# Filter taps built by half steps, one spectrum turn moved behind a scaling, and the last output tile written in four blocks

## What is computed

```
x = x + 0.5 * ffn(layernorm(x))
x = x + attn(layernorm(x))
x = x + 0.5 * ffn(layernorm(x))

ffn(x):  h = silu(x W1' * s1) * (x W2' * s2)        # ternary weights, 256 -> 1024
         h = gelu(h H1' * t1);  h = gelu(h H2' * t2)  # 1024 -> 1024
         return h W3' * s3                            # 1024 -> 256
attn(x): K = 2 Re sum_n C_n exp(dtA_n * t)            # S4D filter, 256 channels x 1024 taps
         y = irfft(rfft(x, 2048) * rfft(K, 2048))[:1024]
         return gelu(y) W' + b
```

## Time and profile before

| what | value |
|---|---|
| median of 3 runs | 1461.65 us (1461.04 to 1462.56) |
| the profiled execution's own time | 1463.29 us |
| its span in the trace | 1461.0 us |
| TensorE busy | 1437.8 us, 98% of the span |
| VectorE busy | 986.4 us, 68% |
| ScalarE busy | 476.6 us, 33% |
| GpSimd busy | 48.1 us, 3% |
| mean granted TensorE clock | 0.998 |

### The profile page before, as it was taken

One profiled execution on the slowest core, in us unless ns is written; L12 is line 12 of the kernel. 1 busy time (PEld: TensorE's weight loads), 2 busy tenths in 40 slices (PEclk: granted clock), 3 DMA queues, 4 the chain that ended last, 5 costly groups with the idle time before them and its releaser, 6 DMA issues.

```text
span 1461.0 us, 17259 instructions
## 1 busy us (share of the span) xinstructions
PE 1437.8 (98%) x6910; PEld 1159.7 (79%) x6910; DVE 986.4 (68%) x1729; ACT 476.6 (33%) x721; POOL 48.1 (3%) x42
## 2 busy tenths in 40 slices
PE   7999999999999999999999999999999999999998
PEld 3688888878777778787887887878878788888886
DVE  7676877684777887858878577784787754353432
ACT  3724342333324324223242242422424223141321
POOL 0000100000000000010000100001000010000000
PEclk9999999999999999999999999999999999999999
DMA  9000000002114121031210312013120112010000
GB/s 362 15 1 29 29 30 29 15 30 72 40 44 144 44 87 55 14 130 44 87 33 26 126 59 72 19 54 97 59 73 15 58 40 72 0 44 0 30 0 16
DMA packets 52545, 80.27 MB, mean 55 GB/s; under 512 B 2672, under 2 KB 44528, under 8 KB 50928
## 3 DMA queue, kind: packets, MB, share of 16 engines
q1 hardware_dynamic: 52464, 79.15, 16.1%
HBM read 57.12 MB, written 22.02 MB: 54 GB/s over the span
## 4 chain that ended last, share of the span: by engine, by line
PE 92%; DVE 6%; ACT 1%; issue 1%; DMA 0%; POOL 0%; DVEq 0%; ACTq 0%; POOLq 0%
PE ps L1249 76%; PE ps L1311 8%; PE ps L1344 3%; PE ps L1397 2%; PE ps L1240 1%; DVE hid_b_lo L1175 1%; PE ps L1338 1%; PE ps L1339 1%; DVE pt L829 1%; PE ps L1387 0%; DVE hid_b_hi L1173 0%; ACT act_o L476 0%; DVE low L1140 0%; DVE tab L832 0%; DVE gr L832 0%
## 5 line engine op out<-in xcount | busy, mean ns | idle before, releaser
L476 ACT ACTIVATE act_o<-ps,scales 128x512 f32<-128x512 f32 x384 | 264.2, 689 | 908.1 <-PE ps L1249 905.3
L1249 PE MATMUL ps<-hid_b_hi,h 128*128 128x512 f32 x1024 | 404.4, 395 | 0.5 <-DVE hid_b_lo L1175 0.3
L1249 PE MATMUL ps<-hid_b_lo,h 128*128 128x512 f32 x1024 | 401.6, 392 | 0.0
L1249 PE MATMUL ps<-hid_a_hi,h 128*128 128x512 f32 x992 | 393.1, 396 | 0.2
L1249 PE MATMUL ps<-hid_a_lo,h 128*128 128x512 f32 x992 | 388.7, 392 | 0.0
L1249 PEld LDWEIGHTS ps<-hid_b_hi,h 128*128 128x128 f32 x1024 | 192.5, 188 | 44.8 <-DVE hid_b_lo L1175 1.4
L1249 PEld LDWEIGHTS ps<-hid_b_lo,h 128*128 128x128 f32 x1024 | 192.5, 188 | 43.1 <-issue 1.2
L1249 PEld LDWEIGHTS ps<-hid_a_hi,h 128*128 128x128 f32 x992 | 186.3, 188 | 47.5 <-DVE hid_a_lo L1166 2.8
L1249 PEld LDWEIGHTS ps<-hid_a_lo,h 128*128 128x128 f32 x992 | 186.4, 188 | 41.4 <-issue 2.2
L1249 PE MATMUL ps<-hid_b_hi,w 128*128 128x512 f32 x480 | 190.3, 396 | 2.1 <-DVE gz L1226 2.1
L1249 PE MATMUL ps<-hid_b_lo,w 128*128 128x512 f32 x480 | 189.6, 395 | 0.0
(11 more groups left out here) (246 smaller groups left out, 1237.9 us busy)
## 6 DMA issues: line engine op xcount, KB each, us to landing
ks<-k_d SPq DMA_DIRECT2D x32, 512.0 KB, 3.8
raws<-in_weights SPq DMA_DIRECT2D x11, 1024.0 KB, 15.5
gz<-in_x SPq DMA_DIRECT2D x8, 512.0 KB, 3.7
xin<-in_x SPq DMA_DIRECT2D x8, 512.0 KB, 3.9
x_d<-xin SPq DMA_DIRECT2D x8, 512.0 KB, 2.9
z_d<-xin SPq DMA_DIRECT2D x8, 512.0 KB, 2.9
k_d<-ks SPq DMA_DIRECT2D x8, 512.0 KB, 2.6
zb<-z_d SPq DMA_DIRECT2D x8, 512.0 KB, 5.2
```

The lines of the kernel that those rows point to most:

```text
L476: A(act_o[:, k % ACT_SLOTS], bank(source), func, scale=scale).then_inc(s_act, 1)
L1249: last = MM(o, weight[:, k, cols].bitcast(dt), part[:, k].bitcast(dt), start=(k == 0 and i == 0), stop=(k == n - 1 and i == len(act_) - 1))
```

## The change

1. `MADE` is replaced by `TABLES` and `FACTORS`: the two halves of a piece (the table, the factors) now stand at steps of their own, and `make_factors` is split into `make_table` and `make_factors`. `MASKED` and `MULTIPLIED` move with them. The last multiplication is at step 21 of tile 3 instead of 17, and so is the copy-out of the sums (L581) with the SyncE transfers behind it. The next tile's norm in tile 3 is at steps 19 and 20 instead of 17 and 18.
2. `turn(7)` stands behind the scaling L1226 of tile 4, ahead of the addition L1230. `finish_taps(7)` stands behind the first silu of tile 5.
3. Tile 15's last layer is `layer_three_last`. Its four sums go to banks 4 to 7, one per block, and it does not wait for step 23's activation but for the filter's last use of these banks. Blocks 0 and 1 run their first seven k-steps before anything that needs step 23. VectorE then scales and adds each block by itself (128x256), and SyncE stores each block by itself (128 KB).

```
-    if T == 3:
-        return 17, 18
-    if T == 4:
+    if T in (3, 4):
         return 19, 20
...
-MADE = {(2, 17): 0, (2, 19): 1, (2, 21): 2, (3, 8): 3, (3, 9): 4, (3, 10): 5, (3, 11): 6, (3, 14): 7}
-MULTIPLIED = {(2, 20): 0, (2, 22): 1, (3, 8): 2, (3, 11): 3, (3, 12): 4, (3, 13): 5, (3, 14): 6, (3, 17): 7}
+TABLES = {(2, 17): 0, (2, 19): 1, (2, 21): 2, (2, 23): 3, (3, 9): 4, (3, 11): 5, (3, 15): 6, (3, 17): 7}
+FACTORS = {(2, 18): 0, (2, 20): 1, (2, 22): 2, (3, 8): 3, (3, 10): 4, (3, 14): 5, (3, 16): 6, (3, 18): 7}
+MULTIPLIED = {(2, 21): 0, (2, 23): 1, (3, 8): 2, (3, 11): 3, (3, 13): 4, (3, 17): 5, (3, 19): 6, (3, 21): 7}
...
-            store_x(ALL - 1)
-            sp.wait_ge(s_xst, 16 * ALL)
+            for j in range(J):
+                sp.wait_ge(s_x, ALL + j)
+                sp.dma_start(rows(out, TILES - 1)[:, j], xin[:, j]).then_inc(s_xst, 16)
+            sp.wait_ge(s_xst, 16 * (ALL - 1 + J))
...
-                if T == 3 and k == 17:
+                if T == 3 and k == 21:
                     act.wait_ge(s_tap, PIECES)
...
                 for m in range(KH):
                     hidden(T, m, ACT.Silu, scales[:, 0, m:m + 1])
+                    if T == 5 and m == 0:
+                        finish_taps(7)
...
                 if T == 4:
-                    for i in (6, 7):
-                        finish_taps(i)
+                    finish_taps(6)
...
-                if (T, k) in MADE:
-                    make_factors(MADE[T, k])
+                if (T, k) in TABLES:
+                    make_table(TABLES[T, k])
+                if (T, k) in FACTORS:
+                    make_factors(FACTORS[T, k])
...
+            def make_table(n):
+
+                if n >= 2:
+                    dve.wait_ge(s_tap, n - 1)
+                step(powers_product(tab[:, n % 2], n, uim, ure, 0))
+
+            def make_factors(n):
+
+                if n:
+                    dve.wait_ge(s_masked, n)
+                powers_product(gr[:, :, :], n, ure, uim, 1).then_inc(s_factor, 1)
...
                 if T == 4:
                     turn(6)
-                    turn(7)
...
+                if T < ALL - 1:
+                    dve.wait_ge(s_o, T + 1)
+                    V.tensor_tensor(gz[:, :, :], bank(2, 2).rearrange("p (j d) -> p j d", j=J),
+                                    s3[:, :].unsqueeze(1).to_broadcast([P, J, D]), ALU.mult).then_inc(s_upd, 1)
+                    if T == 4:
+                        turn(7)
...
+            dve.wait_ge(s_xr, 16 * ALL)
+            for j in range(J):
+                dve.wait_ge(s_o, ALL + j)
+                V.tensor_tensor(gz[:, j], ps[:, 4 + j, 0:D], s3[:, :], ALU.mult).then_inc(s_upd, 1)
+                dve.wait_ge(s_upd, ALL + j)
+                V.tensor_tensor(xin[:, j], xin[:, j], gz[:, j], ALU.add).then_inc(s_x, 1)
...
+            def layer_three_last(dt):
+
+                T = ALL - 1
+                pe.wait_ge(s_x2, B)
+
+                def steps_of(j, first, last_):
+                    for k in range(first, last_):
+                        pe.wait_ge(s_split, at_split(T, 2 * KH + k))
+                        for i, part in enumerate((hid_a_hi, hid_a_lo)):
+                            last = MM(ps[:, 4 + j, 0:D], part[:, k, j * P:(j + 1) * P].bitcast(dt), w3[:, k].bitcast(dt),
+                                      start=(k == 0 and i == 0), stop=(k == KH - 1 and i == 1))
+                    return last
+
+                for j in range(2):
+                    steps_of(j, 0, KH - 1)
+                for j in range(J):
+                    steps_of(j, KH - 1 if j < 2 else 0, KH).then_inc(s_o, 1)
```

More of the change, by code:

```diff
@@ L133, in norm2_at @@
     return (20, 21) if 4 < T <= TILES else (-1, -1)
[L138 to L140 removed]
+TABLES = {(2, 17): 0, (2, 19): 1, (2, 21): 2, (2, 23): 3, (3, 9): 4, (3, 11): 5, (3, 15): 6, (3, 17): 7}
+FACTORS = {(2, 18): 0, (2, 20): 1, (2, 22): 2, (3, 8): 3, (3, 10): 4, (3, 14): 5, (3, 16): 6, (3, 18): 7}
+MASKED = {(2, 19): 0, (2, 21): 1, (2, 23): 2, (3, 9): 3, (3, 11): 4, (3, 15): 5, (3, 17): 6, (3, 19): 7}
+MULTIPLIED = {(2, 21): 0, (2, 23): 1, (3, 8): 2, (3, 11): 3, (3, 13): 4, (3, 17): 5, (3, 19): 6, (3, 21): 7}
 def norm_calls():
@@ L810, in prepare, with powers_product @@
                     step(V.scalar_tensor_tensor(uim[:, 0], uim[:, 0], col(C_IM), xt[:, 1], ALU.mult, ALU.add))
-                if (T, k) in MADE:
-                    make_factors(MADE[T, k])
+                if (T, k) in TABLES:
+                    make_table(TABLES[T, k])
+                if (T, k) in FACTORS:
+                    make_factors(FACTORS[T, k])
             def lift(i):
                 return x12[:, i].unsqueeze(2).to_broadcast([P, P, NU])
-            def make_factors(n):
+            def powers_product(out_, n, x, y, i):
@@ L819, in make_factors @@
                 q = slice(n * PIECE, (n + 1) * PIECE)
                 wide = [P, PIECE, NU, NV]
[L821 to L836, removed]
+                out_, extra = (t.rearrange("p q (u v) -> p q u v", v=NV) for t in (out_, pt[:, :, :]))
@@ new lines, in powers_product @@
+                for to, u, v in ((out_, x, vre), (extra, y, vim)):
+                    last = V.tensor_tensor(to, u[:, i, q].unsqueeze(3).to_broadcast(wide),
+                                           v[:, i, q].unsqueeze(2).to_broadcast(wide), ALU.mult)
+                step(last)
+                return V.tensor_tensor(out_, out_, extra, ALU.add)
+            def make_table(n):
+                if n >= 2:
+                    dve.wait_ge(s_tap, n - 1)
+                step(powers_product(tab[:, n % 2], n, uim, ure, 0))
@@ L1222, in _ @@
                     update(second_of(T))
-                dve.wait_ge(s_o, T + 1)
                 if T == 0:
                     dve.wait_ge(s_s3, 1)
[L1226 to L1230, removed]
+                if T < ALL - 1:
[4 more added lines that the diff above has]
+                        turn(7)
+                    dve.wait_ge(s_upd, T + 1)
+                    dve.wait_ge(s_xr, 16 * (T + 1))
+                    V.tensor_tensor(xin[:, :, :], xin[:, :, :], gz[:, :, :], ALU.add).then_inc(s_x, 1)
+            dve.wait_ge(s_xr, 16 * ALL)
[4 more added lines that the diff above has]
+                V.tensor_tensor(xin[:, j], xin[:, j], gz[:, j], ALU.add).then_inc(s_x, 1)
         @block.tensor
@@ L1437, in feed_forward @@
                         project(second_of(T))
-                    layer_three(T, dt)
+                    if T + 1 < ALL:
+                        layer_three(T, dt)
+                layer_three_last(dt)
             pe.wait_ge(s_ident, 16)
```

## The result

The changed kernel takes 1454.45 us in the median of 4 runs (1453.2 to 1456.95), the kernel before 1462.1 us (4 runs, 1461.04 to 1462.56). The ratio is 0.9947, 95% interval 0.9936 to 0.9959: faster by 7.65 us, where 6.5 were forecast. Measured again beside its parts it is 1455.82 against 1462.47 us, 6.65 us.

What follows compares the result with a forecast made beforehand. TensorE, busy 98% of the span, bounds the kernel, so only its waits, slow stretches and the work behind its last matmul count. Taps 2.2, turn 0.8 and end 3.5 sum to 6.5 us: 1461.65 - 6.5 = 1455.1, range 1453.2 to 1457.3.

Steps and rivals of the forecast that it cites:

- Taps: Tile 3, steps 11 to 16: tap multiplications no longer wait for masks; gain 2.2 us, bounds 1.6 and 2.4.
- The cover of the mirror matmuls: Time between the tap sums' landing and the mirror matmuls needing them: shrinks from 16 us to 1.3 or more, costing nothing.
- Rival D: Mirror's input late, from 1.3 us of delay on: slower, 1464.6 us, chance 0.02; 0.04 that it takes part of the gain.
- The moved turn: Tile 5's start: the gap is cut in two, worth nothing by itself; clock saving 0.8 us, bounds 0 and 1.75.
- the slow stretch: Tile 5, behind TensorE's 2.09 us gap: granted clock 0.95 over 35 us, avoiding it saves up to 1.75 us.
- Rival A: Tile 5's start: the clock falls as before, behind the second gap; gain 5.7 us, time 1455.9, chance 0.3.
- The end: Last layer and store: 0.78 us from the wait, 1.62 from VectorE, 1.1 from the smaller store; 3.5 us together.
- Rival B: Last store: fixed cost takes its whole gain, or four issues delay the end; end gives 2.4, 1456.2 us, chance 0.1.
- Rivals C and E: C: tile 3's tap stalls stay, 1457.3 us, chance 0.05; E: a tap entry or last layer still waits, 1458.8, 0.03.
- The sum: Whole kernel: 2.2 + 0.8 + 3.5 = 6.5 us faster, 1455.1 us against the median.

Runs made afterwards that it cites:

- changed, again: The changed kernel with no edit, measured once more beside its parts: 1455.82 us, ratio 0.9955 to the kernel before.
- turn(7) moved: The changed kernel with turn(7) alone moved, in halves behind two gates of tile 5: 1454.44 us, ratio 0.9948 to the kernel before.

## Why the prediction was right, point by point

- **Taps.** 2.2 us forecast, 2.23 in the first profiles (89.03 to 86.80), 2.2 to 2.3 between kernels with and without the part. The halves fit because 3.11 us of VectorE stand against 3.665.
- **The cover of the mirror matmuls.** "1.3 or more" was forecast and 1.3 measured, by taking a step away. Rival D's mechanism is real and sat one step from deciding; its price was under-stated. The prediction has "each us late one us lost", but a wait of 2.34 us cost 2.9 to 3.5 by the tile, with the clock at half behind it.
- **The moved turn.** "The reordering by itself is worth nothing" holds within 0.1 us. The idle pieces were 0.52 and 1.44, forecast 0.5 and 1.8: the records show step 1 as 2.1 us of work where 1.83 was taken, and from its start to step 2's it was 3.56 us, forecast 3.62. In the profile the term was 1.5 us of the 1.75 (93.27 to 91.78), 1.3 of it the slow stretch. For the median 0.8 was taken, the middle between two values because nothing could decide; the part alone gave 0.75, with an interval of 0.3 to 2.9. That the two agree is luck and confirms no step of the reasoning. Rival A did not occur in any of the six profiles that have the two pieces, and the 2.09 us piece let the clock fall in two of three.
- **The end.** 0.78 and 1.62 us forecast; from the last gelu's start to VectorE's end there were 1457.69 - 1446.88 = 10.81 us before and 8.42 after, 2.39 less. For the store 1.1 was forecast and 1.2 measured where no engine was late. Rival B (the fixed cost eats the gain) falls with the two kernels that changed the stores alone. The Trainium skill's advice to coalesce many small transfers into one large (DMA: Bandwidth & Descriptors, "Rules for kernel authors") doesn't hold where the last transfer is on the path: 1.7 us from issue to landing for 128 KB against 2.9 for 512. And the "~2 µs" of fixed cost in the same page's "Latency and other measured facts" is too much here, where 128 KB took 1.7 us with its data; that is why the end gained 1.2 by the store and not the 0.9 which the prediction worked out from the page.
- **Rivals C and E.** No step of tile 3 is held up, and the last layer starts without a wait; both fall with the first profile after.
- **The sum.** 6.5 us forecast, 7.65 and 6.65 measured; both lie in the range. By the profiles the terms are 2.2 for the taps, 2.4 + 1.2 for the end and 0.1 for the reordering, 5.9 us, and 1.3 more in executions in which the slow stretch stood before. The medians are coarser than that: the three parts alone add up to 3.1 + 0.75 + 4.8 = 8.7 us, 2 us more than the whole measured beside them. So the terms are confirmed by the tiles and the end, and the sum only to 1 or 2 us.
- **What the prediction took wrongly.** It laid the spread of the timed runs to the slow stretch at tile 5. More of it is the clock at another place, the start. The stretch from the first transposes to those at the end of tile 0 took 94.0 to 96.0 us in the 13 profiles. TensorE starts at half its rate there, and how long that lasts differs: the first matmuls of 128x512 begin 0.85 us apart until 18.65 us in the kernel before and until 15.24 in "changed, again", and 0.43 apart from then on. TensorE's groups in 15 to 18 and in 15.6 to 18 us (count, busy us, mean ns):

```profile
L1249 PE MATMUL ps<-zf,raws 128*128 128x512 f32 x5 | 4.4, 1050 | 0.0
```
```profile
L1263 PE MATMUL ps<-zf,raws 128*128 128x512 f32 x7 | 3.3, 605 | 0.0
```

Each trace's first record of the full clock lies between 15.4 and 18.8 us, and the later it is, the longer is tile 0 (93.99 us with the earliest, 95.59 and 95.96 with the two latest). At half the rate 3.4 us more cost 1.7 of the 2.0 us between the extremes; "turn(7) moved" has besides 0.5 us more waiting for the first weights than the others. The late engine adds 1.6 to 2 us in two profiles.

## What to carry to other kernels

Where one engine is nearly always busy, look for what stands on another engine's queue ahead of the instruction it waits for, and ask for the next wait behind that one: cutting a gap in two by reordering is worth next to nothing by itself until the sum of the work ahead of the last of the waits falls; it can still keep the clock up: the clock fell in none of six profiles with the gap cut in two, and in two of three with the gap whole. Threaded side work fits if each piece plus the step's own work stays under the step's length; halves over more steps of 3.67 us did that at no cost for the taps, as long as their consumer was still behind them by more than a transfer, while the halves of turn(7) in steps of 1.84 us gave back 0.6 of 1.4 us. When executions of one kernel differ by a few us, compare them stretch by stretch, the start first. At a program's end, split the last scaling and store so that only the last block's are on the path.

## What was not expected of the hardware

The granted clock went to 0.5 behind a gap of only 2.09 us in two executions and stayed at 1.0 behind the same gap in a third; a gap of 2.34 us brought it down, two of 0.5 and 1.4 us with 2.1 us of work between did not in six. The full clock came at 15.4 us in one execution and at 18.8 in another, with the same work ahead of it. The last store's landing is 1.7 us for 128 KB, but in 2 of 13 profiles one DMA engine was still at its packets 1.5 us or more after the others were done, and both times its share began as a 16 KB packet of the `instruction` queue ended.
